# Transposes of the normalized rows by transfers and VectorE, in a macaron block of FFN, linear attention and FFN

## The chip, the cores and the metric

The kernel runs on one core of one Trainium2 chip. The metric is the device time of one execution in microseconds (us); times given are medians over runs.

## What is computed

The input is x, 4096 tokens of 256 features (two sequences of 2048). The reference, cut to what matters:

```
x = x + 0.5 * ffn(layernorm(x))          # FFN stage 1
x = x + attn(layernorm(x))               # linear attention, 16 heads of 16
x = x + 0.5 * ffn(layernorm(x))          # FFN stage 2

ffn(x):  x_prev = x shifted by one token
         xr = mu_r*x + (1-mu_r)*x_prev ;  xk = mu_k*x + (1-mu_k)*x_prev
         return sigmoid(xr @ W_r.T) * (square(relu(xk @ W_k.T)) @ W_v.T)
attn(x): q = relu(x Wq)/4 ; k = relu(x Wk)/4 ; v = x Wv ; u = silu(x Wu)
         kv = sum over tokens of k v, per head ; out = q kv
         return (head_norm(out) * u) @ Wo.T
```

## The kernel before

The tokens are cut into 8 blocks of 512 (4 tiles of 128 tokens). `FFN` numbers the work: n = 0 to 7 is stage 1 on block n, n = 8 to 15 is stage 2 on block n - 8. There is no scheduler: each engine's program is written out by hand, in order, and engines wait for one another only by semaphores. So an instruction that waits holds back all that stands behind it on its engine.

The change lies in the loops `for i in range(1, 7)` that every engine has. Iteration i does the projections of FFN i, prepares the mixed rows of FFN i+1, and does the attention projections of block i-1. TensorE (PE) does in iterations 2 to 6: `ffn_k(i)`, `transpose_a(i+1)`, `transpose_b(i-1)`, `ffn_r(i)`, `k_and_u(i-1)`, `ffn_v(i)`, `gram(i-1)` and `q_of(i-1)`; from i = 5 on also `attend`, in i = 6 `transpose_g(0)` and `project_out(0)`. Every product is three fp32r matmuls (high by high, low by high, high by low), so each operand needs a high and a low part, which other engines make.

What the steps of the prediction touch:

- `transpose_a(n)` (L1300, L1310): eight 128x128 transposes on PE from the normalized rows `xn` (tokens on partitions) to PSUM `psA` (features on partitions). ScalarE's `previous(n)` (L636, L642) and VectorE's `mix_current(n)` (L957) read `psA`.
- The rows of `xn` come from ScalarE's `normalize(n)` (L625), which waits for `s_lnA >= 3*n`, that is for GpSimd's `scales_a(n)` (L405 to L417: `var_epsA`, `rstdA`, `mean_rstdA`, `shiftA`). Its statistics are VectorE's `stats_a(n)` (`bn_rows`, `bn_all`).
- ScalarE in iteration i: `front` = `activate_k(i)` (relu and square of both halves, L685, L692), `x2_high(i-1)` (L720), `previous(i+1)`, `sigmoid_r`, `mix_high`; then `sigmoid_u` four times (L739, L746) with two `kt_high` (L730), `mix_high(i+1, 1)`, `normalize(i+2)`, `x1_high`, `relu_q`.
- VectorE in iteration i: `stats_a(i+2)`, `x2_low(i-1)` (L1033), `mix_current(i+1)`, four `silu` (L1039), then `gate_ffn`/`add_ffn1` twice (L1020, L1027), `stats_b(i)` (L948, L951), `r_low`, `keep_g`; from i = 5 on `gate_heads` and `head_norms` (the Newton steps, L1099 to L1119).
- GpSimd (POOL) in iteration i: `act_low(i)` (L446, L455), `k_low(i+1)` (L433), `kt_low(i-1)` (L485), `scales_a(i+2)`, `scales_b(i)` (L421 to L426, waits for `stats_b(i)`), `x1_low(i)` (L476); in i = 2 also `wo_lo` (L552).
- `gram(i-1)` on PE waits for the two halves of `kt_low`, the second one at its third tile (L1463). `k_and_u(i-1)` waits for `x2_low`; `project_out(0)` waits for VectorE's `g_low(0)` (L1047).
- SyncE (SP) loads x and the weights, then stores: `load_x`, `store_x`.

## Time and profile before

| | |
|---|---|
| time, median of 3 runs | 312.24 us (310.92 to 312.5) |
| the profiled execution | 310.67 us, its span 308.9 us |
| granted TensorE clock | 1.00 throughout |
| PE, PEld (weight load) busy | 301.8 us (98%), 275.2 us (89%) |
| VectorE, ScalarE, GpSimd busy | 240.9 (78%), 235.5 (76%), 215.1 (70%) |
| DMA | 10.85 MB, nearly all before 20 us and after 230 us |

The page gives the busy time of each engine and its share of the span; a busy share is a mean over stages. Which wait ends last in a stage is read from the instructions in order of time, and times in those rows are in us from the span's start. The profiled execution took 1.8 us more than its span.

### The profile page before, as it was taken

How to read it: one execution, taken by the hardware profiler on the slowest of the kernel's cores; microseconds unless marked ns; L12 is line 12 of the kernel's file. 1: busy time of each engine (PE TensorE's matmuls, PEld its weight loads, DVE VectorE, ACT ScalarE, POOL GpSimd, SP SyncE). 2: the span in 40 equal slices, each digit the busy share in tenths (PEclk: the TensorE clock that was granted, in tenths of full speed). 3: DMA queues.
4: the chain of work that ended last, by engine and by line, in shares of the span. 5: the costliest groups of instructions: out<-in, count | busy, mean ns of one | idle time of the engine just before them, and what ended most of it. 6: DMA issues, size and time to landing. Idle time of an engine off the chain costs nothing.

```text
span 308.9 us, 5806 instructions
## 1 busy us (share of the span) xinstructions
PE 301.8 (98%) x2035; PEld 275.2 (89%) x2035; DVE 240.9 (78%) x585; ACT 235.5 (76%) x461; POOL 215.1 (70%) x237
## 2 busy tenths in 40 slices
PE   6999999999999999999999999999999999999995
PEld 4888889988988998998988998989999999999984
DVE  5899875666856946985994799596989797999695
ACT  3979669699589679679269358579797979699981
POOL 4598978789687686669278315726797979758823
PEclk9999999999999999999999999999999999999999
DMA  7960000000000000000000000000001011101123
GB/s 217 382 217 3 0 1 2 2 0 0 3 0 3 0 0 2 0 2 0 0 3 1 2 0 0 2 1 3 0 3 68 11 59 36 35 2 68 39 100 136
DMA packets 10752, 10.85 MB, mean 35 GB/s; under 512 B 482, under 2 KB 10724, under 8 KB 10724
## 3 DMA queue, kind: packets, MB, share of 16 engines
q1 hardware_dynamic: 10432, 10.23, 9.6%
q8 instruction: 16, 0.26, 0.4%
q10 hardware_dynamic: 292, 0.26, 0.2%
q14 instruction: 12, 0.10, 0.1%
HBM read 6.29 MB, written 4.19 MB: 34 GB/s over the span
## 4 chain that ended last, share of the span: by engine, by line
PE 74%; DVE 14%; ACT 4%; POOL 3%; issue 2%; DMA 1%; DVEq 0%; ACTq 0%
PE psK L1293 7%; PE psK L1295 7%; PE psK L1294 7%; PE psX L1293 7%; PE psX L1295 7%; PE psX L1294 7%; PE psRV L1293 6%; PE psRV L1294 6%; PE psRV L1295 6%; DVE mix L957 3%; PE psA L1310 3%; PE psA L1498 2%; PE psX L1511 2%; PE psX L1425 2%; PE psK L1498 2%
## 5 line engine op out<-in xcount | busy, mean ns | idle before, releaser
L957 DVE SCALAR_TENSOR_TENSOR mix<-psA,mu,mix 128x512 f32<-128x512 f32 x60 | 41.5, 745 | 10.0 <-ACT mix L642 10.0
L625 ACT ACTIVATE xn<-xs,shiftA,rstdA 128x256 f32<-128x256 f32 x53 | 27.7, 607 | 16.3 <-POOL shiftA L417 16.3
L433 POOL TENSOR_TENSOR mix_k_lo<-mix,mix_k_hi 128x512 fp32r<-128x512 f32 x26 | 33.2, 1299 | 8.2 <-ACT mix_k_hi L675 8.2
L642 ACT ACTIVATE mix<-psA,one_mu 128x511 f32<-128x511 f32 x60 | 36.9, 697 | 0.0
L1293 PE MATMUL psRV<-ffn_hi,mix_r_hi 128*128 128x256 f32 x120 | 34.3, 286 | 0.0
L1295 PE MATMUL psRV<-ffn_hi,mix_r_lo 128*128 128x256 f32 x120 | 33.6, 280 | 0.0
L1294 PE MATMUL psRV<-ffn_lo,mix_r_hi 128*128 128x256 f32 x120 | 33.5, 279 | 0.0
L1293 PE MATMUL psRV<-ffn_hi,act_hi 128*128 128x256 f32 x96 | 27.5, 287 | 0.2 <-POOL act_lo L455 0.2
L1294 PE MATMUL psRV<-ffn_lo,act_hi 128*128 128x256 f32 x96 | 26.8, 280 | 0.0
L1295 PE MATMUL psRV<-ffn_hi,act_lo 128*128 128x256 f32 x96 | 26.8, 279 | 0.0
L485 POOL TENSOR_TENSOR k_lo<-k_tok,k_hi 128x512 fp32r<-128x512 f32 x14 | 18.1, 1292 | 11.5 <-ACT k_hi L730 11.5
L926 DVE BATCH_NORM_STATS2 statsA<-xs 128x6 f32<-128x256 f32 x64 | 22.5, 415 | 2.5 <-DMA xs<-x_dram 2.4
L1293 PE MATMUL psK<-mix_k_hi,ffn_hi 128*128 128x512 f32 x60 | 24.2, 403 | 0.0
L476 POOL TENSOR_TENSOR x_lo<-xs,x_hi 128x512 fp32r<-128x512 f32 x14 | 17.8, 1295 | 8.6 <-ACT x_hi L725 8.6
L1295 PE MATMUL psK<-mix_k_hi,ffn_lo 128*128 128x512 f32 x60 | 23.6, 393 | 0.0
L1294 PE MATMUL psK<-mix_k_lo,ffn_hi 128*128 128x512 f32 x60 | 23.4, 391 | 0.0
L1293 PEld LDWEIGHTS psRV<-ffn_hi,mix_r_hi 128*128 128x128 f32 x120 | 22.5, 188 | 0.5 <-issue 0.2
L1294 PEld LDWEIGHTS psRV<-ffn_lo,mix_r_hi 128*128 128x128 f32 x120 | 22.6, 188 | 0.2
L1295 PEld LDWEIGHTS psRV<-ffn_hi,mix_r_lo 128*128 128x128 f32 x120 | 22.5, 187 | 0.0
L1033 DVE TENSOR_TENSOR x_lo<-psX,x_hi 128x512 fp32r<-128x512 f32 x16 | 10.3, 685 | 14.4 <-ACT x_hi L720 14.4
L675 ACT ACTIVATE mix_k_hi<-mix 128x512 fp32r<-128x512 f32 x30 | 19.0, 660 | 1.9 <-DVE mix L957 1.8
L1293 PEld LDWEIGHTS psRV<-ffn_hi,act_hi 128*128 128x128 f32 x96 | 18.0, 188 | 0.7 <-POOL act_lo L455 0.4
(210 smaller groups left out, 1081.3 us busy)
## 6 DMA issues: line engine op xcount, KB each, us to landing
xs<-x_dram SPq DMA_DIRECT2D x7, 512.0 KB, 7.8
out_dram<-xs SPq DMA_DIRECT2D x7, 512.0 KB, 2.9
out_dram<-xs SPq DMA_DIRECT2D x4, 128.0 KB, 1.8
xs<-x_dram ACTq DMA_DIRECT2D x2, 128.0 KB, 2.8
xs<-x_dram SPq DMA_DIRECT2D x2, 128.0 KB, 2.6
silu_u<-w_ffn_k_dram SPq DMA_DIRECT2D x1, 256.0 KB, 4.7
silu_u<-w_ffn_r_dram SPq DMA_DIRECT2D x1, 256.0 KB, 5.8
q_store<-w_k_dram SPq DMA_DIRECT2D x1, 256.0 KB, 6.0
```

The source lines that it names most:

```text
L433: nc.gpsimd.tensor_tensor(mix_k_lo[:, h, :], mix[:, 0, h, :], mix_k_hi[:, h, :].bitcast(F32), ALU.subtract).then_inc(s_lo_k, 1)
L476: nc.gpsimd.tensor_tensor(x1_lo[:, g * BANK:(g + 1) * BANK], row(xs, a, g * BANK, BANK), x1_hi[:, g * BANK:(g + 1) * BANK].bitcast(F32), A ...
L485: nc.gpsimd.tensor_tensor(k_lo[:, tiles, :], k_tok[:, tiles, :], k_hi[:, tiles, :].bitcast(F32), ALU.subtract).then_inc(s_kt_lo, 1)
L625: nc.scalar.activation(xn[:, t, :], tile_row(xs, b, t), ACT.Identity, bias=shiftA[:, t:t + 1], scale=rstdA[:, t:t + 1]).then_inc(s_xn, 1)
L642: nc.scalar.activation(mix[:, rk, h, 1:BLOCK], psA[:, h, 0:BLOCK - 1], ACT.Copy, scale=one_mu[:, rk, h:h + 1]).then_inc(s_prev, 1)
L675: nc.scalar.activation(hi[:, h, :], mix[:, rk, h, :], ACT.Identity).then_inc(done, 1)
L926: nc.vector.bn_stats(statsA[:, t, :], tile_row(xs, b, t)).then_inc(s_bnA, 1)
L957: nc.vector.scalar_tensor_tensor(out=m, in0=psA[:, h, :], scalar=mu[:, rk, h:h + 1], in1=m, op0=ALU.mult, op1=ALU.add).then_inc(s_mix, 1)
L1293: nc.tensor.matmul(dst, a_hi, b_hi, start=start, stop=False)
L1294: nc.tensor.matmul(dst, a_hi, b_lo, start=False, stop=False)
L1295: return nc.tensor.matmul(dst, a_lo, b_hi, start=False, stop=stop)
L1498: last = nc.tensor.matmul(ps[:, t // 2, (t % 2) * D + h * P:(t % 2) * D + (h + 1) * P], q_half(j, h)[:, tok(t)], kv_bd[:, j // BB, h, :], ...
```

## The change

For n = 3 to 7 `transpose_a(n)` is gone from PE. In its place:

- SyncE waits for the normalized rows of n (and, for n = 4 to 6, for the transposes of n-1 by VectorE; for n = 7 for the weight means) and issues 16 transfers that move 32-row bands of the rows to other partitions, each 32 partitions x 8 x 32 elements. They land in `squares` (n < 7) or `wsum` (n = 7).
- VectorE's new `turn(n)` waits for them and does two 32x32-block transposes of 128x512 into `psA`. For n = 3 it stands behind `x2_low(1)` in iteration 2, for n = 4 to 6 at the head of iteration n-1, for n = 7 at the end of iteration 5.
- The normalized rows of n = 4 and 6 are written to `gout` instead of `xn`.
- Statistics of n = 5 to 7 move one iteration earlier on VectorE: the four `bn_stats` stand between the `silu` calls, `bn_all` behind `stats_b`.
- GpSimd: `scales_a(i+2)` stands ahead of `act_low(i)` for i = 2 to 5 (for i = 1 between `act_low(1)` and `k_low(2)`). `act_low(6)` now stands ahead of `norm_second(0)`.
- ScalarE: for i = 2 to 6 `x2_high` stands between the two halves of `activate_k(i)`. `normalize(4)` stands behind them in iteration 2, ahead of `previous`. In iterations 3 to 5 tiles 0 and 1 of `normalize(i+2)` stand ahead of `activate_k(i)` and tiles 2 and 3 behind it.
- VectorE's `head_norms(0)` moves from the end of iteration 5 to iteration 6, between `x2_low(5)` and `mix_current(7)`; only its sums stay in iteration 5.

```diff
+        TURNED = range(3, 8)
+        QUAD = 32
+        QUADS = P // QUAD
...
+        def turned_before(n):
+            return 2 * n - 2 * (n in TURNED and n > TURNED[0])
@@ block.sync
+            for n in TURNED:
+                sp.wait_ge(*normalized(n, TILES - 1))
+                if n == 7:
+                    sp.wait_ge(s_wmean, 4)
+                elif n > TURNED[0]:
+                    sp.wait_ge(s_tA, 2 * n)
+                for j in range(QUADS):
+                    for i in range(QUADS):
+                        rows = quads_of(n)[j * QUAD:(j + 1) * QUAD, i * D:(i + 1) * D]
+                        sp.dma_start(rows.rearrange("c (th f) -> c th f", f=QUAD),
+                                     rows_of(n)[i * QUAD:(i + 1) * QUAD, :, :].rearrange(
+                                         "c t (h j f) -> c (t h) j f", h=HALVES, j=QUADS)[:, :, j, :]
+                                     ).then_inc(s_quads[n % 2], 16)
@@ block.gpsimd
             for i in range(1, 6):
+                if i > 1:
+                    scales_a(i + 2)
                 act_low(i)
+                if i == 1:
+                    scales_a(3)
                 k_low(i + 1)
                 if i > 1:
                     kt_low(i - 1)
-                scales_a(i + 2)
                 scales_b(i)
                 x1_low(i)
...
+            act_low(6)
             norm_second(0)
-            act_low(6)
@@ block.scalar, front(i, nxt, a)
-                activate_k(i)
-                if a is not None and i > 1:
+                    activate_k(i)
+                else:
+                    if i in (3, 4, 5):
+                        normalize(i + 2, (0, 1))
+                    activate_k(i, (0,))
                     x2_high(a)
+                    activate_k(i, (1,))
+                    if i == 2:
+                        normalize(4)
+                    elif i < 6:
+                        normalize(i + 2, (2, 3))
...
-                if i <= 5:
-                    normalize(i + 2)
+                if i == 1:
+                    normalize(3)
@@ block.vector
+            def turn(n, free=()):
+                for s, v in free:
+                    dve.wait_ge(s, v)
+                dve.wait_ge(s_halo, n + 1)
+                dve.wait_ge(s_quads[n % 2], 16 * QUADS * QUADS * ((n - TURNED[0]) // 2 + 1))
+                blocks = quads_of(n).rearrange("p (i t h f) -> p h t i f", i=QUADS, t=TILES, h=HALVES)
+                for h in range(HALVES):
+                    nc.vector.transpose(psA[:, h, :].rearrange("p (t i c) -> p t i c", t=TILES, i=QUADS),
+                                        blocks[:, h, :, :, :]).then_inc(s_tA, 1)
...
-                if 1 < i <= 5:
-                    stats_a(i + 2)
+                if i == 2:
+                    stats_a(4)
+                if 3 <= i <= 5:
+                    turn(i + 1, {4: [(s_wcen, 4)], 5: [(s_kvbd, 1)]}.get(i, ()))
                 if i > 1:
                     x2_low(i - 1)
+                if i == 2:
+                    turn(3)
+                if i == 6:
+                    head_norms(0, True)
                 mix_current(i + 1)
...
-                projections(i - 1)
+                projections(i - 1, i + 3 if 2 <= i <= 4 else None)
...
                 stats_b(i)
+                if 2 <= i <= 4:
+                    bn_all(i + 3)
...
-                    head_norms(i - 5)
+                if i == 5:
+                    for g in range(2):
+                        head_sums(0, g)
+                    turn(7, [(s_gu, 2)])
+                elif i == 6:
+                    head_norms(1)
@@ block.tensor
-                transpose_a(i + 1, [(s_wcen, 4)] if i == 4 else [])
...
-            transpose_a(6, [(s_kvbd, 1)])
...
-            transpose_a(7, [(s_gu, 2)])
```

How the order moves at two places. ScalarE, from the end of iteration 2 into iteration 3, before (`q_store` is `relu_q(1)`, `act_k` and `act_hi` are `activate_k(3)`, `x_hi<-psX` is `x2_high(2)`, `mix` is `previous(4)`):

```order
L752 ACTIVATE q_store<-psX 128x512 [waits s_q] x2
L685 ACTIVATE act_k<-psK 128x512 [waits s_act_lo,s_k]
L692 ACTIVATE act_hi<-act_k 128x512 [waits s_v,s_relu]
L685 ACTIVATE act_k<-psK 128x512 [waits s_k]
L692 ACTIVATE act_hi<-act_k 128x512 [waits s_relu]
L720 ACTIVATE x_hi<-psX 128x512 [waits s_q,s_tB]
L720 ACTIVATE x_hi<-psX 128x512 [waits s_tB]
L636 ACTIVATE mix<-halo 128x4 [waits s_halo,s_lo_r,s_lo_k]
```

and the same place in the changed kernel:

```order
L787 ACTIVATE q_store<-psX 128x512 [waits s_q] x2
L660 ACTIVATE xn<-xs,shiftA,rstdA 128x256 [waits s_tA,s_lnA]
L660 ACTIVATE xn<-xs,shiftA,rstdA 128x256
L720 ACTIVATE act_k<-psK 128x512 [waits s_act_lo,s_k]
L727 ACTIVATE act_hi<-act_k 128x512 [waits s_v,s_relu]
L755 ACTIVATE x_hi<-psX 128x512 [waits s_q,s_tB]
L755 ACTIVATE x_hi<-psX 128x512 [waits s_tB]
L720 ACTIVATE act_k<-psK 128x512 [waits s_k]
L727 ACTIVATE act_hi<-act_k 128x512 [waits s_relu]
L660 ACTIVATE xn<-xs,shiftA,rstdA 128x256 [waits s_tA,s_lnA]
L660 ACTIVATE xn<-xs,shiftA,rstdA 128x256
L671 ACTIVATE mix<-halo 128x4 [waits s_halo,s_lo_r,s_lo_k]
```

Two tiles of `normalize(5)` with their wait for `s_lnA` now stand ahead of `activate_k(3)`, two behind it and ahead of `previous(4)`.

GpSimd, from the end of iteration 2 into iteration 3, before (`var_epsB` to `rstd2B` is `scales_b(2)`, `x_lo` is `x1_low(2)`, then `act_low(3)`):

```order
L421 TENSOR_SCALAR var_epsB<-meanvarB 128x4 [waits s_aggB]
L424 TENSOR_TENSOR rstdB<-var_epsB,minus_half 128x4 [waits s_mvB]
L426 TENSOR_TENSOR rstd2B<-rstdB 128x4 [waits s_lnB]
L476 TENSOR_TENSOR x_lo<-xs,x_hi 128x512 [waits s_x1hi] x2
L552 TENSOR_TENSOR wo_lo<-wo,wo_hi 128x512 [waits s_wo_hi]
L446 TENSOR_TENSOR act_k<-act_k 128x512 [waits s_act_hi] x2
```

and in the changed kernel:

```order
L453 TENSOR_SCALAR var_epsB<-meanvarB 128x4 [waits s_aggB]
L456 TENSOR_TENSOR rstdB<-var_epsB,minus_half 128x4 [waits s_mvB]
L458 TENSOR_TENSOR rstd2B<-rstdB 128x4 [waits s_lnB]
L508 TENSOR_TENSOR x_lo<-xs,x_hi 128x512 [waits s_x1hi] x2
L587 TENSOR_TENSOR wo_lo<-wo,wo_hi 128x512 [waits s_wo_hi]
L440 TENSOR_SCALAR var_epsA<-meanvarA 128x4 [waits s_aggA]
L445 TENSOR_TENSOR rstdA<-var_epsA,minus_half 128x4 [waits s_xn,s_mvA]
L447 TENSOR_TENSOR mean_rstdA<-meanvarA,rstdA 128x4 [waits s_lnA]
L449 TENSOR_SCALAR shiftA<-mean_rstdA 128x4 [waits s_lnA]
L478 TENSOR_TENSOR act_k<-act_k 128x512 [waits s_act_hi] x2
```

`scales_a(5)`, whose last instruction writes `shiftA`, now stands behind `scales_b(2)`, `x1_low(2)` and `wo_lo`, ahead of `act_low(3)`.

## Rows read from the trace of the kernel before

**Rows 1.** The page: granted clock in 40 slices, and the chain that ended last, by engine
```profile
PEclk9999999999999999999999999999999999999999
...
PE 74%; DVE 14%; ACT 4%; POOL 3%; issue 2%; DMA 1%; DVEq 0%; ACTq 0%
```

**Rows 2.** Iterations 2, 4, 6 (length; PE, PEld, DVE, ACT, POOL busy; clock)
```profile
43.78:64.99 21.21, 21.21 (x137) 19.05 (x136) 13.34 (x33) 16.83 (x34) 16.17 (x17) 1.00 0.01 2
...
86.86:109.14 22.28, 22.28 (x145) 20.02 (x145) 14.15 (x34) 17.73 (x35) 16.61 (x18) 1.00 0.00 1
...
132.24:158.96 26.72, 26.72 (x185) 24.63 (x184) 21.91 (x52) 17.35 (x34) 15.88 (x15) 1.00 0.01 2
```

**Rows 3.** TensorE in order of time, iteration 2: start us, length us, engine, line
```profile
46.51 1.04 PE L1310 MATMUL psA<-ident,xn 128*128 128x128 f32 x8
47.38 1.04 PE L1425 MATMUL psX<-ident,xs 128*128 128x128 f32 x8
```

**Rows 4.** ScalarE in order of time, iteration 2 (idle time and its releaser in brackets)
```profile
45.34 0.60 ACT L685 ACTIVATE act_k<-psK 128x512 f32<-128x512 f32 x1 [0.76 <-PE psK L1295]
45.97 0.63 ACT L692 ACTIVATE act_hi<-act_k 128x512 fp32r<-128x512 f32 x1
...
48.02 1.09 ACT L720 ACTIVATE x_hi<-psX 128x512 fp32r<-128x512 f32 x2
48.98 0.21 ACT L636 ACTIVATE mix<-halo 128x4 f32<-128x4 f32 x1
...
56.78 0.47 ACT L739 ACTIVATE k_tok<-psK,rstd2B 128x256 f32<-128x256 f32 x1 [0.48 <-PE psK L1295]
57.16 0.47 ACT L746 ACTIVATE silu_u<-psK,rstdB 128x256 f32<-128x256 f32 x1
57.51 0.63 ACT L730 ACTIVATE k_hi<-k_tok 128x512 fp32r<-128x512 f32 x1
...
61.90 2.08 ACT L625 ACTIVATE xn<-xs,shiftA,rstdA 128x256 f32<-128x256 f32 x4 [2.72 <-POOL shiftA L417]
```

**Rows 5.** VectorE in order of time, iteration 2
```profile
57.66 0.48 DVE L1039 SCALAR_TENSOR_TENSOR silu_u<-psK,rstdB,silu_u 128x256 f32<-128x256 f32 x1 [0.83 <-ACT silu_u L746]
58.20 0.69 DVE L1020 SCALAR_TENSOR_TENSOR gate<-psRV,gate 128x512 f32<-128x512 f32 x1
```

**Rows 6.** GpSimd in order of time, iteration 2
```profile
58.22 1.30 POOL L485 TENSOR_TENSOR k_lo<-k_tok,k_hi 128x512 fp32r<-128x512 f32 x1 [1.27 <-ACT k_hi L730]
59.60 0.52 POOL L408 TENSOR_SCALAR var_epsA<-meanvarA 128x4 f32<-128x4 f32 x1
...
63.20 0.55 POOL L421 TENSOR_SCALAR var_epsB<-meanvarB 128x4 f32<-128x4 f32 x1 [1.33 <-DVE meanvarB L951]
...
65.39 2.55 POOL L476 TENSOR_TENSOR x_lo<-xs,x_hi 128x512 fp32r<-128x512 f32 x2
67.89 1.28 POOL L552 TENSOR_TENSOR wo_lo<-wo,wo_hi 128x512 fp32r<-128x512 f32 x1
```

**Rows 7.** TensorE in order of time, end of iteration 5
```profile
124.89 0.28 PE L1293 MATMUL psK<-k_hi,x_hi 128*128 128x256 f32 x1
...
127.71 1.95 PE L1498 MATMUL psA<-kv_bd,q_store 128*128 128x128 f32 x16
```

**Rows 8.** VectorE in order of time, end of iteration 5 and iteration 6
```profile
132.79 1.27 DVE L1099 SCALAR_TENSOR_TENSOR head_ss<-var_epsB,head_ss 128x64 f32<-128x64 f32 x1
...
137.11 1.29 DVE L1033 TENSOR_TENSOR x_lo<-psX,x_hi 128x512 fp32r<-128x512 f32 x2 [0.28 <-ACT x_hi L720]
...
147.13 1.29 DVE L1047 TENSOR_TENSOR g_lo<-psX,g_hi 128x512 fp32r<-128x512 f32 x2 [0.52 <-ACT g_hi L768]
```

**Rows 9.** DMA issues: engine, count, KB each, median us from issue to landing
```profile
out_dram<-xs SPq DMA_DIRECT2D x7, 512.0 KB, 2.9
out_dram<-xs SPq DMA_DIRECT2D x4, 128.0 KB, 1.8
```

**Rows 10.** SyncE's queue in order of time: start, length of one issue
```profile
3.22 0.47 SPq L369 DMA_DIRECT2D q_store<-w_k_dram  x1
```

More of the change, by code:

```diff
@@ L168, in macaron @@
         s_tA = sem("s_tA")
+        s_quads = [sem(f"s_quads_{k}") for k in range(2)]
         s_prev = sem("s_prev")
@@ L294, in prev_part, with quads_of, rows_of @@
             return mix_part(n, rk, h) + n
+        TURNED = range(3, 8)
+        QUAD = 32
+        QUADS = P // QUAD
+        def quads_of(n):
+            return (squares[:].rearrange("p g e -> p (g e)") if n < 7
+                    else wsum[:].rearrange("p n e -> p (n e)"))
+        def rows_of(n):
+            return gout if n in TURNED and n % 2 == 0 else xn
+        def turned_before(n):
+            return 2 * n - 2 * (n in TURNED and n > TURNED[0])
         def half(g):
@@ L620, in normalize @@
                 if n > 0:
-                    act.wait_ge(s_tA, 2 * n)
+                    act.wait_ge(s_tA, turned_before(n))
                 for t in tiles:
@@ L624, in normalize @@
                         continue
-                    nc.scalar.activation(xn[:, t, :], tile_row(xs, b, t), ACT.Identity,
+                    nc.scalar.activation(rows_of(n)[:, t, :], tile_row(xs, b, t), ACT.Identity,
                                          bias=shiftA[:, t:t + 1], scale=rstdA[:, t:t + 1]).then_inc(s_xn, 1)
@@ L1186, in _, with projections @@
             ffn_weight_low(2)
-            def projections(a):
+            def projections(a, n=None):
                 for t in range(TILES):
+                    if n is not None:
+                        bn_rows(n, (t,))
                     silu(a, t)
             for i in range(1, 7):
-                if 1 < i <= 5:
-                    stats_a(i + 2)
+                if i == 2:
+                    stats_a(4)
+                if 3 <= i <= 5:
+                    turn(i + 1, {4: [(s_wcen, 4)], 5: [(s_kvbd, 1)]}.get(i, ()))
                 if i > 1:
                     x2_low(i - 1)
+                if i == 2:
+                    turn(3)
+                if i == 6:
+                    head_norms(0, True)
                 mix_current(i + 1)
```

## The prediction

> **What bounds the kernel now.** I read the page first: the chain that ended last runs 74% on PE, at full granted clock [rows 1]. The stretches of iterations 2, 4 and 6 come next: PE is busy for all of each, and they last 21.21, 22.28 and 26.72 us [rows 2]; their edges give the starts of iterations 2, 4 and 6 (43.78, 86.86 and 132.24 us). So PE binds, and every instruction taken from it shortens the kernel, but only while the others keep up. Their own order of time is what matters then. ScalarE runs from 45.34 to 58.14 in iteration 2 with a single idle spot that a wait on PE makes, 0.48 us at 56.78; its large idle time, 2.72 us, lies just before `normalize`, where it waits for `shiftA` [rows 4]. GpSimd works through `k_lo`, `scales_a`, `scales_b`, `x_lo` and `wo_lo` [rows 6]. The reader should see that the wait for `shiftA` stood where ScalarE had time to spare.
>
> **What is taken from PE.** Eight transposes take 47.38 - 46.51 = 0.87 us [rows 3]. Five blocks give 5 x 0.87 = 4.35 us, all of it on the path as long as nobody else is late. That is the most the change can win.
>
> **The transfers.** 80 of them, 16 for each block. One issue on SyncE takes 0.47 us [rows 10], so 16 take 7.5 us; the last lands 1.8 us later if it takes as long as a store of 128 KB [rows 9]: 9.3 us. Their pieces are 32 elements, 128 bytes, 4096 of them for 512 KB, eight times as many as in a store of the same 512 KB (rows of 256 elements), which took 2.9 us. If time goes by pieces this is at most 8 x 2.9 = 23.2 us; if by bytes, 2.9 us and the issues bind. I take 9.3 us, since each issue is a short row and the store is the nearest one. `normalize(3)` keeps its place in iteration 1; one iteration before 61.90 + 2.08 [rows 4] is 42.8, and its `scales_a` no longer stands behind two low parts of 1.3 us [rows 6], so its rows are ready near 40 us (an estimate), and `turn(3)` can start near 49: just covered. At 23.2 us `turn(3)` would be 14 us late, once; later blocks have some 20 us each, by the times below, so the cover holds for them or is short by little.
>
> **VectorE's new work.** Ten block transposes of 128x512. The trace shows none; the cheapest 128x512 row is about 0.65 us, twice that is the upper end: 1.4 to 2.7 us for a pair [nearest: rows 5, `gate`, 0.69]. I take 1.4. They lie where VectorE waited for `x2_high`, so I cost them at nothing; without that cover it would be 1.4 us an iteration. The statistics between the `silu` calls fill gaps such as the 0.83 us before 57.66 [rows 5].
>
> **What the moved steps do.** In iterations 3 to 5 the first two tiles of `normalize(i+2)` stand ahead of `activate_k(i)` on ScalarE, and wait for `shiftA`. On GpSimd `scales_a(i+2)` now stands behind `x1_low(i-1)`. In the old trace GpSimd leaves `x1_low(2)` at 67.89 and `wo_lo` at 69.17 [rows 6], while iteration 3 starts at 64.99, the end of the stretch of iteration 2 [rows 2]. So `shiftA` comes several us after the point where ScalarE used to begin `activate_k` (1.56 us into iteration 2: 45.34 against 43.78 [rows 2, 4]). All that ScalarE does for PE stands behind it.
>
> First `shiftA(5)`, on the old clock. Relu and square of half 0 from 45.34; `x2_high(1)` starts 0.64 us into `transpose_b`, as before (48.02 - 47.38), which now begins at 46.51: 47.15. It takes 0.96 (to 48.98), half 1 takes 1.27 (0.64 + 0.63), all four tiles of `normalize(4)` 2.0: `previous(3)` starts at 51.38 instead of 48.98 [rows 3, 4]. From there to the end of the last sigmoid was 57.63 - 48.98 less the 0.48 idle: 8.17 us, dense, so 59.55. Then `silu` to `gate` 0.57 (58.20 - 57.63) [rows 5]; `gate` to `scales_b` 5.00 (63.20 - 58.20); `scales_b` 2.19; `x1_low` 2.50; `wo_lo` 1.23 to 1.28; `scales_a` 2.30 (61.90 - 59.60) [rows 4, 6]. Sum: 73.3 us.
>
> Then each `shiftA` follows from the one before, round a loop of three engines, none of which has idle time in it:
>
> normalize two tiles 1.0 + half 0 1.27 + `x2_high` 0.96 + half 1 1.27 + two tiles 1.0 + `previous` to last sigmoid 8.17 + 0.57 + 5.00 + 2.19 + 2.50 + 2.30 = 26.2 us.
>
> Two rounds: `shiftA(7)` at 73.3 + 52.4 = 125.7. From it the end of iteration 5: 5.5 us (the first five terms) to `previous(6)`, 8.68 to the end of the second `kt_high` (58.14 - 48.98, less 0.48, plus rounding), 0.08 + 1.30 for the second `kt_low` [rows 4, 6], then PE's last three quarters of `gram` (3/4 of 127.71 - 124.89 = 2.12) and `attend` with `q_of`, 132.24 - 127.71 = 4.53 [rows 2, 7]: 125.7 + 5.5 + 8.68 + 1.38 + 2.12 + 4.53 = 147.9. Iteration 6 thus begins 15.7 us late (132.24 before). The four times 0.87 us that PE has saved by then are in that figure: PE now waits.
>
> **Iteration 6** has no `normalize`. It saves its 0.87 us but `head_norms(0)` now stands ahead of `mix_current(7)` on VectorE. The steps filled 132.79 to 136.83 (137.11 less 0.28 idle), 4.0 us, of which the first took 1.27 us where its twins take 0.2 to 0.3: 3.0 to 4.0 [rows 8]. `x2_low` now ends 2.73 + 0.64 + 0.63 + 1.29 = 5.3 us into the iteration (`transpose_b` at 2.73, the rest as in [rows 3, 4, 8]), so the mix starts at 8.3 to 9.3. From the end of `x2_low` to the end of `g_low` it was 148.42 - 138.40 = 10.0 us, about 0.9 of it waiting (0.52 at `g_low` itself): 9.1, so `g_low` ends at 17.4 to 18.4. PE reached `project_out` when `g_low` was ready, 16.2 to 16.5 us in, and comes 0.87 earlier now, at 15.6: a stall of 1.8 to 2.8, a net loss of 0.9 to 1.9. I take 1.3. Moving `norm_second(0)` behind `act_low(6)` costs nothing: PE needs it only after `k_and_u`.
>
> **Sum.** 15.7 + 1.3 = 17 us. The profiled execution took 310.67 us, so 327.7; the median of the runs shown is 1.6 us above it, which gives 329.
>
> **Where the Trainium skill bears on it.** A store of 128 KB took 1.8 us from issue to landing [rows 9]. The Trainium skill, DMA: Bandwidth & Descriptors, Rules for kernel authors, says that under 64 KB one pays mostly overhead and should coalesce small transfers; each one here is 32 KB. By that rule this change is the wrong way round; the trace agrees only as far as 128 KB takes 1.8 us where 512 KB takes 2.9. It gives rival B below. In the trace the clock stands at 1.00 with PE never idle [rows 1, 2]. The Trainium skill, TensorE: Matmul & The Clock Gate, Why this matters for your kernels, warns that idle gaps of PE bring the clock back down; no run here shows it, and it gives rival C.
>
> **The rivals.**
> A, faster: `scales_a` comes early enough that ScalarE never waits. Its statistics are indeed ready an iteration sooner. It decides at the point where `shiftA` comes no later than 1.0 us ahead of the old start of `activate_k`, 0.6 us into the iteration. Then the 4.35 us stay: 310.67 - 4.35 = 306.3, 307.9 as a median. Against it stand the rows of GpSimd: it leaves `x1_low` 2.9 us into iteration 3 and needs 2.3 more. Chance 0.04.
> A', the delay comes once and does not go round the loop, because engines behind it have slack that I don't see: some 5 us at iteration 3 and 2 at iteration 2, less 4.35: 310.67 + 2.65 + 1.6 = 315. Chance 0.04.
> B, the transfers do not overlap: 16 x 1.8 = 28.8 us for each block. Then the loop runs through transfers and `turn`, 28.8 + 1.4 = 30.2 us for each of n = 4 to 7, and `turn(3)` is at 40 + 28.8 = 68.8, done at 70.2. `turn(7)` comes at 70.2 + 4 x 30.2 = 191, where I expect it near 150: 40 us more, 369. Half-way cases (23.2 us a block) cost `turn(3)` some 13 us: 342. Chance 0.09 together.
> C, the clock falls to its lower level (1.2 GHz) in the gaps that PE now has, about 26.2 - (22.28 - 0.87) = 4.8 us in each of iterations 3 to 5. Most of the slower matmuls are hidden in the loop; only the last 6.65 us of iteration 5 are on the path, and as much again in iteration 6: up to 7 us more, 333 to 336. Chance 0.09.
>
> **How the numbers follow.** Forecast 0.74: 329 us, own range 323 to 335 (1 us for iteration 6, the rest for what of the loop is looser or tighter than its rows, four rounds at 1 us). A and A' lie below 318, B above 338; C lies inside. Range 318 to 338. A measurement here can tell 0.5% (1.6 us) from no change. Faster 0.04 (A), same 0.02 (between A and A'), slower 0.94.
>
> **What would show it.** `shiftA` of blocks 5, 6 and 7 some 26 us apart; ScalarE's largest wait at `normalize` for `shiftA`, about 4 to 6 us, three times; PE idle before `k_and_u` in iteration 3 for `x2_low` and before the third tile of `gram` for `k_lo`; iterations 3 to 5 at 25 to 28 us instead of 22 to 23; the transfers of a block landed within 10 us. I am wrong if ScalarE does not wait there, if VectorE waits for the transfers, or if the granted clock falls.

## The result, and the profile after

| | before | changed |
|---|---|---|
| median (lowest to highest), us | 311.58 (310.41 to 312.5) | 331.54 (330.66 to 332.14) |
| ratio, 95% interval | 1 | 1.0641 [1.0592, 1.0689] |
| profiled execution / its span, us | 310.67 / 308.9 | 331.65 / 329.9 |

The changed kernel is 6.4% slower; the forecast was 329, with a range of 318 to 338. Of all the runs below one is left out, of the kernel with the Newton steps back: 338.75 us at a mean granted clock of 0.849, against 324.67 to 325.4 us in its others. The changed kernel's page answers to [rows 1]: TensorE's clock shows two dips, and only half of the chain that ended last is TensorE's.

```profile
PE 305.6 (93%) x1995; PEld 275.8 (84%) x1995; DVE 250.1 (76%) x595; ACT 235.3 (71%) x461; POOL 213.6 (65%) x237
PEclk9999999998999999999979999999999999999999
...
PE 49%; DVE 17%; ACT 15%; POOL 9%; issue 5%; SPq 3%; DMA 1%; POOLq 0%; ACTq 0%; DVEq 0%
```

Iterations 2 to 6 as stretches, cut where TensorE begins `ffn_k(i)` (columns as in [rows 2]; the third figure is the length):

```profile
46.04:70.37 24.33, 21.36 (x128) 18.43 (x128) 17.06 (x45) 18.15 (x36) 16.68 (x21) 1.00 0.22 37
70.37:97.52 27.15, 22.89 (x131) 19.87 (x131) 16.00 (x38) 17.18 (x35) 17.41 (x19) 0.94 0.12 20
97.52:123.18 25.66, 22.22 (x137) 19.32 (x137) 15.32 (x36) 17.04 (x34) 15.94 (x18) 1.00 0.13 22
123.18:148.61 25.43, 22.96 (x148) 20.37 (x147) 15.84 (x32) 17.40 (x35) 15.69 (x18) 1.00 0.13 21
...
148.61:180.16 31.55, 27.51 (x178) 25.20 (x176) 25.25 (x55) 17.27 (x34) 15.96 (x15) 0.95 0.00 1
```

Iterations 3 and 5 of the kernel before, from the view of [rows 2]:

```profile
64.99:86.86 21.87, 21.87 (x139) 19.44 (x139) 14.76 (x36) 18.09 (x36) 17.86 (x21) 1.00 0.01 1
...
109.14:132.24 23.10, 23.10 (x155) 21.07 (x154) 16.50 (x39) 17.61 (x35) 16.54 (x18) 1.00 0.00 1
```

Before, the five lasted 21.21, 21.87, 22.28, 23.10 and 26.72 us, 115.18 together; now 134.12. That is 18.9 of the 21.0 us between the spans. The rest is in front: iteration 1 began at 22.86 us here and at 20.75 in the execution shown of before. It began near 22.9 in 3 of the 14 profiled executions of this study and between 20.6 and 21.1 in the others, so I put these 2 us down to the execution and not to the change. How many of the timed runs began late is not known. Below, kernels are compared by the sum of iterations 2 to 6 in their traces, and by the timed runs.

ScalarE in order of time at the head of iterations 3, 4 and 5, where [rows 4] had `act_k` at once:

```profile
69.92 0.60 ACT L787 ACTIVATE q_store<-psX 128x512 f32<-128x512 f32 x1 [0.63 <-PE psX L1363]
76.07 1.09 ACT L660 ACTIVATE xn<-xs,shiftA,rstdA 128x256 f32<-128x256 f32 x2 [5.55 <-POOL shiftA L449]
77.07 0.57 ACT L720 ACTIVATE act_k<-psK 128x512 f32<-128x512 f32 x1
...
101.35 1.09 ACT L660 ACTIVATE gout<-xs,shiftA,rstdA 128x256 f32<-128x256 f32 x2 [4.29 <-POOL shiftA L449]
...
126.63 1.09 ACT L660 ACTIVATE xn<-xs,shiftA,rstdA 128x256 f32<-128x256 f32 x2 [4.29 <-POOL shiftA L449]
```

GpSimd, which makes `shiftA`:

```profile
68.37 0.19 POOL L453 TENSOR_SCALAR var_epsB<-meanvarB 128x4 f32<-128x4 f32 x1 [3.68 <-DVE meanvarB L994]
...
70.22 2.55 POOL L508 TENSOR_TENSOR x_lo<-xs,x_hi 128x512 fp32r<-128x512 f32 x2
72.71 1.30 POOL L587 TENSOR_TENSOR wo_lo<-wo,wo_hi 128x512 fp32r<-128x512 f32 x1
74.09 0.20 POOL L440 TENSOR_SCALAR var_epsA<-meanvarA 128x4 f32<-128x4 f32 x1
...
75.84 0.19 POOL L449 TENSOR_SCALAR shiftA<-mean_rstdA 128x4 f32<-128x4 f32 x1
...
101.12 0.19 POOL L449 TENSOR_SCALAR shiftA<-mean_rstdA 128x4 f32<-128x4 f32 x1
...
126.40 0.20 POOL L449 TENSOR_SCALAR shiftA<-mean_rstdA 128x4 f32<-128x4 f32 x1
```

From `shiftA` of block 5 to that of block 6, and from there to that of block 7, it is 25.28 us, twice to the hundredth. That is how a closed loop without idle time looks. TensorE stands behind it. Its longest waits in the whole span (total in us, times, longest), apart from one of 2.6 us at the very start that the kernel before has too:

```profile
PE psX L1361 <- DVE x_lo L1086: 5.4, 3, 3.2
PE psK L1361 <- POOL k_lo L517: 5.0, 6, 1.0
PE psX L1579 <- DVE silu_u L1092: 4.0, 1, 4.0
```

The third is not of the loop: `transpose_g(0)` in iteration 6 waits for the `silu` products, behind the Newton steps. Nor are the losses of iteration 2 (3.1 us), where ScalarE normalizes the four tiles of block 4 ahead of `previous(3)` and TensorE then waits 1.00 and 0.95 us for `k_lo` and 0.53 us for a sigmoid. No experiment changes this place alone; in the versions a block ahead, which do not have it, iteration 2 lasts 21.3 us.

### The profile page after: what moved, and what is told of

Read it like the earlier page. It is cut to its first block, busy times and chain, and to the rows that moved or that the text cites. A ratio compares the mean times of both kernels' runs of the same rounds, so it can differ in the third digit from the quotient of the medians.

```text
span 329.9 us, 5823 instructions
## 1 busy us (share of the span) xinstructions
PE 305.6 (93%) x1995; PEld 275.8 (84%) x1995; DVE 250.1 (76%) x595; ACT 235.3 (71%) x461; POOL 213.6 (65%) x237
## 4 chain that ended last, share of the span: by engine, by line
PE 49%; DVE 17%; ACT 15%; POOL 9%; issue 5%; SPq 3%; DMA 1%; POOLq 0%; ACTq 0%; DVEq 0%
PE psX L1361 4%; PE psX L1363 4%; PE psX L1362 4%; PE psK L1361 4%; PE psRV L1361 4%; PE psK L1363 4%; PE psRV L1363 4%; PE psK L1362 4%; PE psRV L1362 4%; SPq L406 3%; ACT mix L677 3%; ACT xn L660 2%; POOL x_lo L508 2%; PE psA L1566 2%; DVE mix L1000 2%
## 5 line engine op out<-in xcount | busy, mean ns | idle before, releaser
L660 ACT ACTIVATE xn<-xs,shiftA,rstdA 128x256 f32<-128x256 f32 x45 | 23.8, 610 | 12.5 <-POOL shiftA L449 12.5
L1361 PE MATMUL psRV<-ffn_hi,act_hi 128*128 128x256 f32 x96 | 28.4, 296 | 0.8 <-ACT gate L748 0.5
L1362 PE MATMUL psRV<-ffn_lo,act_hi 128*128 128x256 f32 x96 | 27.5, 287 | 0.0
L1363 PE MATMUL psRV<-ffn_hi,act_lo 128*128 128x256 f32 x96 | 27.5, 286 | 0.0
L1086 DVE TENSOR_TENSOR x_lo<-psX,x_hi 128x512 fp32r<-128x512 f32 x16 | 10.3, 684 | 21.3 <-ACT x_hi L755 21.3
L969 DVE BATCH_NORM_STATS2 statsA<-xs 128x6 f32<-128x256 f32 x64 | 23.4, 414 | 2.3 <-DMA xs<-x_dram 2.1
L478 POOL TENSOR_TENSOR act_k<-act_k 128x512 f32<-128x512 f32 x14 | 14.5, 1046 | 13.3 <-ACT act_hi L727 13.3
L453 POOL TENSOR_SCALAR var_epsB<-meanvarB 128x4 f32<-128x4 f32 x8 | 2.9, 368 | 31.1 <-DVE meanvarB L994 31.1
```

The costliest lines, as they stand in the source:

```text
L478: nc.gpsimd.tensor_tensor(act_k[:, h, :], act_k[:, h, :], act_k[:, h, :], ALU.mult).then_inc(s_sq, 1)
L660: nc.scalar.activation(rows_of(n)[:, t, :], tile_row(xs, b, t), ACT.Identity, bias=shiftA[:, t:t + 1], scale=rstdA[:, t:t + 1]).then_inc(s ...
L969: nc.vector.bn_stats(statsA[:, t, :], tile_row(xs, b, t)).then_inc(s_bnA, 1)
L1361: nc.tensor.matmul(dst, a_hi, b_hi, start=start, stop=False)
L1362: nc.tensor.matmul(dst, a_hi, b_lo, start=False, stop=False)
L1363: return nc.tensor.matmul(dst, a_lo, b_hi, start=False, stop=stop)
```

## The experiments

"Sum" is iterations 2 to 6 in the trace. Before: 115.18; the changed kernel: 134.12.

| kernel | median, us | ratio to before, 95% | sum, us |
|---|---|---|---|
| rows behind | 325.12 | 1.0453 [1.0416, 1.0490] | 129.34 |
| scales first | 323.27 | 1.0384 [1.0344, 1.0424] | 126.31 |
| both | 325.45 | 1.0451 [1.0391, 1.0510] | 127.95 |
| TensorE's transposes | 331.16 | 1.0647 [1.0595, 1.0700] | 134.52 |
| Newton steps back | 324.72 | 1.0447 [1.0397, 1.0496] | 129.88 |
| Newton steps alone | 314.26 | 1.0115 [1.0060, 1.0170] | 117.96 |
| scales first, Newton steps back | 316.37 | 1.0196 [1.0158, 1.0235] | 120.18 |
| a block ahead, 4 to 6 | 309.16 | 0.9948 [0.9921, 0.9975] | 112.68 |
| a block ahead, 4 to 7 | 307.84; again 308.02 | 0.9925 [0.9892, 0.9958]; 0.9918 [0.9893, 0.9944] | 111.94; 111.84 |
| the same, TensorE's transposes | 311.27 | 1.0028 [1.0009, 1.0048] | 114.97 |
| the same, turned twice | 309.30 | 0.9965 [0.9946, 0.9983] | 113.37 |

("GELU" in the recorded expectations stands for `activate_k`, which is relu and square.)

### Is it the transposes or the order?

```diff
-                if 3 <= i <= 5:
-                    turn(i + 1, {4: [(s_wcen, 4)], 5: [(s_kvbd, 1)]}.get(i, ()))
...
+                transpose_a(i + 1, [(s_wcen, 4)] if i == 4 else [])
```

(and so for n = 3, 6 and 7; SyncE's 80 transfers go.)

> Edit: the order of the changed kernel on all engines, but TensorE transposes the rows of blocks 3 to 7 as in the kernel before: no transfers, no transposes on VectorE. Theory (the order costs, not the way of transposing): TensorE has 4.35 us more work, but most of it in iterations in which it waits, so the time is 329 to 335 us, far above 311.6. Rival (the transfers and VectorE's transposes are what costs): the time falls to 310 to 318 us.

331.16 us, as slow as the changed kernel. ScalarE waits 5.53 us for `shiftA` at the head of iteration 3, where it waited 5.55, and the three `shiftA` again lie 25.28 and 25.27 us apart. Transfers, transposes on VectorE and the 4.35 us taken from TensorE together make no difference that can be measured in this order. The rival is refuted: the order costs the whole of it.

### The loop, cut in two ways

Rows behind:

```diff
-                    if i in (3, 4, 5):
-                        normalize(i + 2, (0, 1))
                     activate_k(i, (0,))
                     x2_high(a)
                     activate_k(i, (1,))
-                    if i == 2:
-                        normalize(4)
-                    elif i < 6:
-                        normalize(i + 2, (2, 3))
+                    if i < 6:
+                        normalize(i + 2)
```

> Edit: in iterations 3 to 5 ScalarE normalizes no tile of block i+2 ahead of its GELU of block i; all four tiles come behind it. Theory (the time went into an ordered loop ScalarE - VectorE - GpSimd that comes back to itself through shiftA): the two tiles ahead hold the GELU back by a wait for shiftA of 4 to 6 us and by 1.0 us of work. Without them the loop falls from the 25.3 us measured between two shiftA to about 22.7, so iterations 4 and 5 take 22 to 24 us on TensorE where they took 27.2 and 25.7, and the time is 321 to 326 us, against 331.5 of the changed kernel. Rival (the transfers or VectorE's transposes of the rows cost the time): the transfers start no earlier, the time stays at 329 to 333. Rival (the loop closes another way, for instance through x2_low): the waits move to another wait on GpSimd, and the time falls by under 3 us.

Scales first, on GpSimd:

```diff
             for i in range(1, 6):
-                if i > 1:
-                    scales_a(i + 2)
+                if i == 2:
+                    scales_a(4)
                 act_low(i)
...
                 scales_b(i)
+                if 2 <= i <= 4:
+                    scales_a(i + 3)
                 x1_low(i)
```

> Edit: GpSimd makes the scales of block i+2 directly behind scales_b of the block before, ahead of that iteration's x1_low and wo_lo parts. Theory (loop through shiftA): the 2.5 us of x1_low (and 1.2 of wo_lo) leave the stretch between the previous sigmoid and shiftA; the loop falls from 25.3 to 22 to 23.7 us, ScalarE's wait for shiftA falls from 4 to 6 us to 1 to 3, and the time is 320 to 326 us. Rival (transfers): the rows are ready 2 to 3 us earlier each block, so the time would fall only if turn() was waited for; it was waited for only in the first block, so 329 to 333. Rival (what is pushed back, x2_low, decides): TensorE's wait for x2_low before k_and_u grows and the time stays within 2 us.

325.12 and 323.27 us: 6.4 and 8.3 us less than the changed kernel, with the transfers as they were. In scales first the row on which the theory rests reads

```profile
70.32 1.09 ACT L662 ACTIVATE xn<-xs,shiftA,rstdA 128x256 f32<-128x256 f32 x2 [1.81 <-POOL shiftA L449]
```

where the changed kernel waited 5.55. Both show that the loop through `shiftA` held TensorE. With the rows behind, iterations 4 and 5 took 24.17 and 24.30 us, just over the 22 to 24 expected. (The 27.2 and 25.7 us in that expectation are those of iterations 3 and 4.)

> Edit: both of the above together. Theory: the loop comes to about 20 us, which is under the 21 to 22 us that TensorE itself needs for an iteration, so shiftA is waited for by nobody in iterations 4 and 5, TensorE's iterations 3 to 5 take 21 to 23 us (27.2, 25.7 and 25.4 before), iteration 6 starts at 135 to 139 us in place of 148.6, and the time is 317 to 322 us: what is left over the kernel before is iteration 2 and 3's loss and that of iteration 6. Rival (transfers cost the time): 327 or more. If it comes to the two singles' gains added (some 14 us off) the two were separate delays; if to much less than the sum, TensorE or another engine bounds from about 22 us on.

325.45 us: the expectation failed. With both edits ScalarE no longer waits for `shiftA` in iterations 3 to 5, and yet iterations 4 and 5 last 24.16 and 24.32 us, 1 us more than with scales first alone (its two below):

```profile
93.94:118.10 24.16, 21.94 (x136) 19.26 (x137) 15.32 (x36) 17.15 (x34) 15.90 (x18) 1.00 0.14 23
118.10:142.42 24.32, 22.70 (x147) 20.31 (x146) 15.82 (x32) 17.52 (x35) 15.94 (x17) 1.00 0.14 22
```

```profile
91.77:114.95 23.18, 21.73 (x136) 19.21 (x137) 15.31 (x36) 17.05 (x34) 15.92 (x18) 1.00 0.15 24
114.95:138.27 23.32, 22.43 (x148) 20.24 (x146) 15.83 (x32) 17.52 (x35) 15.96 (x17) 1.00 0.14 23
```

ScalarE of both, in order of time, iteration 4:

```profile
95.63 0.60 ACT L722 ACTIVATE act_k<-psK 128x512 f32<-128x512 f32 x1 [2.14 <-PE psK L1361]
...
99.58 2.07 ACT L662 ACTIVATE gout<-xs,shiftA,rstdA 128x256 f32<-128x256 f32 x4
...
109.41 0.68 ACT L767 ACTIVATE k_hi<-k_tok 128x512 fp32r<-128x512 f32 x1
```

and TensorE, which waits at `gram` for GpSimd's `k_lo`, made from that `k_hi`:

```profile
109.61 0.36 PE L1359 MATMUL psK<-k_hi,x_hi 128*128 128x256 f32 x1 [0.68 <-POOL k_lo L517]
111.49 0.39 PE L1359 MATMUL psK<-k_hi,x_hi 128*128 128x256 f32 x1 [0.96 <-POOL k_lo L517]
```

I read this as a second loop, which I had not seen: `ffn_k`, `act_k`, all that ScalarE does up to the last `k_hi` (nearly dense from 95.63 to 110.09), `k_lo`, `gram`, `g_acc`, `ffn_k`. Its parts add up: 1.69 us to `act_k`, 14.46 on ScalarE, 1.40 to the second half of `gram` at 111.49, 6.61 on TensorE to the next `ffn_k` at 118.10, together 24.16. Rows behind alone has the same iterations 3 to 5 (23.84, 24.17 and 24.30 us against 23.83, 24.16 and 24.32), so there too this loop and not `shiftA` held TensorE: once the rows stand behind, making the scales earlier gains nothing. In scales first only two tiles lie inside this loop, but the first loop is still closed: ScalarE waits about 1.8 us for `shiftA` three times, and the three lie 22.80 and 22.81 us apart. Its 23.2 us are thus no clean measure of the second loop with two tiles. Two tiles ahead of `act_k` would fall into the time in which ScalarE waits for TensorE anyway (2.14 us above) if `shiftA` came early enough; that was not run. By this reading rows do least harm in front of or behind the whole stretch; the versions a block ahead bear it out.

### The Newton steps

Back to the end of iteration 5:

```diff
-                if i == 6:
-                    head_norms(0, True)
                 mix_current(i + 1)
...
                     turn(7, [(s_gu, 2)])
+                    head_norms(0, True)
```

> Edit: in the changed kernel the first heads' Newton steps go back to the end of iteration 5, behind the transposes of block 7's rows. Theory (the steps, placed ahead of mix_current(7), hold up the silu products of block 6 and with them TensorE's transpose_g: iteration 6 took 31.6 us where it took 26.7 before): iteration 6 falls to 26.5 to 28 us, the wait of 4.04 us for silu_u and the low clock behind it go, and the time is 326 to 329 us against 331.5. Rival (iteration 6 is long because block 7 comes late through shiftA): it stays at 30 us or more, and the time at 330 or more. Rival (prediction's size, 0.9 to 1.9 us): 329.6 to 330.6.

The other way round, in the kernel before:

```diff
                 if i > 1:
                     x2_low(i - 1)
+                if i == 6:
+                    head_norms(0, True)
                 mix_current(i + 1)
...
-            norm_second(0)
             act_low(6)
+            norm_second(0)
```

(`head_norms(0)` keeps its sums in iteration 5.)

> Edit: the kernel before, with only the second part of the change: the first heads' Newton steps in iteration 6 behind x2_low(5) and ahead of mix_current(7), and GpSimd's low parts of the activation ahead of the second part of the norms. Theory (the loss of iteration 6 is this step's own, 3.5 to 5 us): 314.7 to 316.6 us against 311.4. Rival (it is the prediction's 0.9 to 1.9 us, and the rest came from the blocks being late): 312.3 to 313.3. Rival (in the order of before the steps are hidden): 310.5 to 312.

Back: 324.72 us, 6.8 less, and below the 326 to 329 expected. Iterations 5 and 6 last 26.93 and 26.29 us in place of 25.43 and 31.55, 3.8 together; TensorE waits for no `silu_u`, and its granted clock in iteration 6 is 1.00 again. In iteration 5 it fell, behind two waits for `k_lo`, of 0.58 and 0.95 us, which the changed kernel has too (0.58 and 0.94) and which show no dip there:

```profile
138.00:142.00 4.00, 3.05 (x18) 2.86 (x18) 3.90 (x7) 0.91 (x2) 1.22 (x1) 0.75 0.26 42
```

The clock is 0.75 in these 4 us and 0.83 in the next 4, which is 1.7 us of full clock, enough for the 1.5 us by which iteration 5 is longer; what set it off is open. By the traces the steps' place costs 3.8 us (iterations 5 and 6 together) to 5.3 us (iteration 6 alone). Of the 6.25 us between the two profiled executions 4.2 lie in iterations 2 to 6 and 2.0 in the later start; the rest of the timed difference can be of that kind. Alone: 314.26 us against 310.61 in the same runs, 3.65 more (expected: 314.7 to 316.6), and 3.03 in iteration 6 (29.75). VectorE in that kernel:

```profile
131.22 1.27 DVE L1081 TENSOR_REDUCE head_ss<-squares 128x32 f32<-128x512 f32 x2
136.84 1.29 DVE L1033 TENSOR_TENSOR x_lo<-psX,x_hi 128x512 fp32r<-128x512 f32 x2 [4.36 <-ACT x_hi L720]
138.05 0.58 DVE L1099 SCALAR_TENSOR_TENSOR head_ss<-var_epsB,head_ss 128x64 f32<-128x64 f32 x1
...
142.32 2.72 DVE L957 SCALAR_TENSOR_TENSOR mix<-psA,mu,mix 128x512 f32<-128x512 f32 x4
```

The 4.36 us that it now waits are the hole that the steps used to fill [rows 8: 132.79 to 136.83]. Behind `x2_low` the same steps have no hole, so the mix begins at 142.32 instead of 138.85, and TensorE stops at `transpose_g(0)`:

```profile
147.57 1.09 PE L1517 MATMUL psX<-ident,gout 128*128 128x128 f32 x8 [2.68 <-DVE silu_u L1039]
```

That settles it: this part of the change costs 3 us or more by itself, in either order. (The edit moves the steps and GpSimd's `act_low(6)` together, as the change does; they were not tried apart.) The two causes add: with scales first and the steps back the traces' sum is 120.18, and the time

> Edit: the changed kernel with GpSimd's scales directly behind scales_b (323.3 us by itself) and with the Newton steps at the end of iteration 5 (325.1 us by itself). Theory (two separate causes, which add): 331.5 - 8.2 - 6.5 = 316.8, so 315.5 to 318 us. What is then left over the kernel before is iteration 2's and 3's loss and what the GELUs behind normalized tiles still cost. Rival (the Newton steps then stand in front of work that the faster loop wants early): 318.5 or more.

316.37 us, as expected. What is left over the kernel before sits in iterations 2 to 4 (23.78, 23.36 and 23.18 us against 21.21, 21.87 and 22.28).

### What the transposes are worth where the order does no harm

The version a block ahead: in the kernel before, every step that prepares a block's rows keeps its slot but works on the next block:

```diff
-                scales_a(i + 2)
+                if i + 3 <= 7:
+                    scales_a(i + 3)
...
-                if i <= 5:
-                    normalize(i + 2)
+                if i + 3 <= 7:
+                    normalize(i + 3)
...
-                projections(i - 1)
+                projections(i - 1, i + 3 if i + 3 <= 7 else None)
...
+                if 3 <= i <= 5:
+                    turn(i + 1, {4: [(s_wcen, 4)], 5: [(s_kvbd, 1)]}.get(i, ()))
...
                     gate_heads(i - 5)
+                    if i == 5:
+                        turn(7, [(s_gu, 2)])
                     head_norms(i - 5)
```

Block 3 stays with TensorE and is normalized and scaled in iteration 1; `projections` takes the next block's `bn_stats` between its `silu` calls; transfers and `turn` are the changed kernel's.

> Edit: the kernel before, in which the rows of blocks 4 to 6 are transposed by transfers and VectorE, and their statistics, scales and normalization run one block further ahead in the slots that they had, so that nothing that waits for shiftA stands ahead of a GELU; the Newton steps as before. Theory (the transfers and VectorE's transposes are harmless; the order cost the time): TensorE is rid of 3 times 0.87 us and waits for nothing new: 307.5 to 310.5 us against 311.4. Rival (the transposes on VectorE, 1.3 us a block, or the issues on the transfer queue delay something in any order): 311 to 315. Rival (a gap in which TensorE did the transposes just opens): 311 to 312.

> Edit: as the one for blocks 4 to 6, with block 7 as well, its VectorE transposes behind gate_heads(0). Theory (as there): another 0.87 us less for TensorE, less up to 0.6 us by which VectorE's work of iteration 6 starts later: 306.5 to 310 us. Rival (the end of iteration 5 and iteration 6 have no room on VectorE for the two transposes of 1.3 us): slower than the version for blocks 4 to 6 by 0.5 to 1.5 us.

309.16 and 307.84 us: both faster than the kernel before, by 0.5% and 0.75%. TensorE has no new wait above 0.2 us (iterations 2 to 6 of the second):

```profile
44.05:65.38 21.33, 21.33 (x136) 19.16 (x137) 14.11 (x35) 18.36 (x39) 17.46 (x19) 1.00 0.15 25
65.38:86.47 21.09, 20.95 (x131) 18.55 (x130) 15.69 (x38) 17.96 (x37) 17.87 (x21) 1.00 0.16 26
86.47:107.99 21.52, 21.45 (x136) 19.14 (x137) 15.09 (x36) 17.41 (x35) 16.60 (x18) 1.00 0.16 27
107.99:130.15 22.16, 22.16 (x148) 20.19 (x147) 16.07 (x32) 15.55 (x31) 14.75 (x14) 1.00 0.14 23
130.15:155.99 25.84, 25.84 (x178) 23.79 (x177) 22.25 (x55) 17.12 (x34) 15.70 (x15) 1.00 0.00 1
```

ScalarE still waits 2.71 us for `shiftA` in iteration 3, but behind the last `k_hi`, where nobody waits for it:

```profile
82.82 2.08 ACT L662 ACTIVATE gout<-xs,shiftA,rstdA 128x256 f32<-128x256 f32 x4 [2.71 <-POOL shiftA L449]
```

Three runs beside each other then separate order and transposes: the same order with TensorE's transposes, the same with VectorE's done twice, and the version itself again.

```diff
                 for h in range(HALVES):
                     nc.vector.transpose(psA[:, h, :].rearrange("p (t i c) -> p t i c", t=TILES, i=QUADS),
+                                        blocks[:, h, :, :, :]).then_inc(s_twice, 1)
+                dve.wait_ge(s_twice, HALVES * (n - TURNED[0] + 1))
+                for h in range(HALVES):
+                    nc.vector.transpose(psA[:, h, :].rearrange("p (t i c) -> p t i c", t=TILES, i=QUADS),
                                         blocks[:, h, :, :, :]).then_inc(s_tA, 1)
```

> Edit: the order of the version for blocks 4 to 7 (statistics, scales and normalization one block further ahead), but TensorE does all transposes: no transfers, none on VectorE. Theory (moving a transpose off TensorE is worth its 0.87 us where TensorE has no gap, and the order itself is worth nothing): 3.5 us above the version with transfers, so 310.5 to 312 us, like the kernel before. Rival (the order, not the transposes, gave the 2.8 us): 307 to 309 us.

> Edit: the version for blocks 4 to 7 in which VectorE transposes each block's two halves twice over, 1.4 us more of VectorE for each of four blocks. Theory (VectorE has room there: it is busy 60 to 75 per cent of those iterations, and TensorE waits for nothing of it): within 0.7 us of the same version without the doubling, with at most the mix of the block coming 1.4 us later. Rival (VectorE's transposes are on the path to mix_current): 1.4 us for each block, some 5 us more.

> Edit: none against the version for blocks 4 to 7, run again beside the three others for a closer figure. Theory: 306.5 to 309 us, and faster than the kernel before by 0.4 to 1.2 per cent. Rival (the first figure of 0.9925 was chance): a ratio of 0.997 to 1.003.

With TensorE's transposes 311.27 us, again 308.02: 3.25 us for four blocks, of 4 x 0.87 = 3.48 possible. The order itself gives nothing: with TensorE's transposes it is 0.28% slower than the kernel before, just clear of noise, and iteration 1, which now prepares block 4 as well, lasts 23.3 us instead of 23.0. The gain of 0.8% is no chance.

Turned twice is 1.3 us slower than the version itself, where I expected at most 0.7. The place is single: iterations 3 to 5 are unchanged (21.12, 21.54, 22.22), iteration 6 lasts 27.14 instead of 25.62 to 25.84, where TensorE now waits 1.08 us for `x2_low`, behind `turn(7)` and the Newton steps. So for blocks 4 to 6 VectorE had 1.3 us free; for block 7 it has none. The expectation had taken VectorE as busy for 60 to 75% of these iterations; in iteration 6 it is busy for 22.25 of 25.84 us.

## Why the prediction was right

**The bound and the gain from TensorE.** TensorE was the bound, and a transposed block is worth its 0.87 us while nobody else is late; shown at 3.25 of 3.48. In the changed kernel the 4.35 us are worth nothing, as said ("PE now waits"). That the loop through `shiftA` would outlast TensorE's own round, and by how much, was right, and it is the larger part of the loss: iteration 6 began 14.3 us late with this execution's start taken off.

**The transfers.** The rows of block 3 were ready near 41 (39 by the start of before), forecast 40. An issue takes longer than the 0.47 us of [rows 10]. SyncE's queue in order of time, and VectorE's first `turn`:

```profile
41.16 11.54 SPq L406 DMA_DIRECT2D squares<-xn  x16
55.50 10.38 SPq L406 DMA_DIRECT2D squares<-gout  x16
...
54.09 1.32 DVE L1010 STREAM_TRANSPOSE psA<-squares 128x512 f32<-128x512 f32 x2 [2.63 <-DMA squares<-xn]
```

Sixteen take 10.4 to 11.5 us, 0.65 to 0.72 each, and a transfer lands 1.9 us after its issue (median): 12 to 13 us a block, not 9.3, inside the bounds of 2.9 and 23.2. The same queue had issues of 0.43 to 0.93 us in the kernel before, so the one row of 0.47 was a narrow basis. `turn(3)` was therefore not "just covered" but waited 2.63 us; that iteration lasts 24.08 us with TensorE's transposes too, so it cost at most 0.25. With that two signs of the list went against the prediction: the transfers did not land within 10 us, and VectorE waited for them, once. Rival B is refuted: the transfers overlap. The Trainium skill (DMA: Bandwidth & Descriptors, Rules for kernel authors) advises against transfers under 64 KB as mostly overhead. The trace agrees as far as the issuing queue goes, which these transfers hold for 0.65 to 0.72 us each. In the versions a block ahead they cost nothing: the same table's advice to issue early and wait late is what these versions do.

**VectorE's transposes.** A pair took 1.32 us, forecast 1.4, hidden.

**`shiftA(5)`** was to be ready at 73.3 us; it was at 76.03, of which 2.1 are the later start of this execution: 73.9.

**The loop** was put at 26.2 us; it is 25.28. Most of that is GpSimd's: `scales_a` takes 1.95 us (from 124.65 to 126.60) for the 2.30 of the sum and `scales_b` 1.85 for 2.19, since their first instructions (`var_epsA`, `var_epsB`) now take 0.19 where [rows 6] had 0.52 and 0.55. **Iteration 6** began at 148.61, or 146.5 with this execution's start taken off, forecast 147.9.

**Iteration 6 itself** is the term that was mis-sized: a net loss of 0.9 to 1.9 us was forecast, "I take 1.3"; it was 4.8. I had the steps at 3.0 to 4.0 us and TensorE's stall at `project_out`. VectorE in order of time:

```profile
153.80 0.21 DVE L1152 SCALAR_TENSOR_TENSOR head_ss<-var_epsB,head_ss 128x64 f32<-128x64 f32 x1
...
154.54 0.95 DVE L1160 SCALAR_TENSOR_TENSOR head_t<-head_t,head_ss 128x64 f32<-128x64 f32 x1
155.52 1.23 DVE L1162 SCALAR_TENSOR_TENSOR head_y<-head_t,head_y 128x64 f32<-128x64 f32 x1
156.79 1.23 DVE L1164 TENSOR_TENSOR head_t<-head_y 128x64 f32<-128x64 f32 x1
...
159.44 2.72 DVE L1000 SCALAR_TENSOR_TENSOR mix<-psA,mu,mix 128x512 f32<-128x512 f32 x4
```

The steps took 5.6 us, from 153.80 to 159.44. That is the mis-sized term: three of these instructions took 0.95, 1.23 and 1.23 us where the others take 0.2, 2.7 us more in all. Each ended 0.1 us behind a pass of GpSimd that was under way when it began (`act_low(6)`, beside which the change puts them):

```profile
154.28 1.12 POOL L478 TENSOR_TENSOR act_k<-act_k 128x512 f32<-128x512 f32 x1 [1.74 <-ACT act_hi L727]
155.37 2.57 POOL L487 TENSOR_TENSOR act_lo<-act_k,act_hi 128x512 fp32r<-128x512 f32 x2
```

From the start of the mix to the end of `g_low` (168.42) it took 9.0 us, where the forecast had 9.1. So by the forecast's own path `g_low` ended 19.8 us into the iteration instead of 17.4 to 18.4, a stall of 4.2 us and a net loss of 3.3 instead of 1.3. The other 1.5 us are the clock, to which the forecast gave nothing (rival C, below). TensorE also stopped in another place, at `transpose_g(0)`, for 4.04 us; I had followed the chain from the mix to `g_low`, and not asked which of TensorE's instructions first reads anything made behind the mix. In time this made no difference by itself: with `ffn_v(6)` at its old length TensorE would have reached `project_out` at 168.44, when `g_low` was ready.

The forecast of 329 came near to 331.5 by some luck: iteration 6 cost 3.5 us more than forecast, the loop 0.9 us a round less.

**The rivals.** A and A' are refuted: ScalarE waited 4.3 to 5.6 us three times, once a round, as in the list of signs. C was half right, and the list has a falling clock as a sign of being wrong. TensorE's granted clock over the stretches behind its two long waits (the first figure behind the engines' busy times is the clock):

```profile
80.00:84.00 4.00, 3.74 (x10) 2.96 (x11) 1.43 (x3) 4.00 (x9) 3.50 (x3) 0.57 0.10 17
...
164.00:168.00 4.00, 3.32 (x20) 3.32 (x21) 2.33 (x5) 4.00 (x11) 2.57 (x2) 0.71 0.02 4
168.00:172.00 4.00, 4.00 (x32) 4.00 (x32) 3.53 (x6) 0.62 (x2) 0.00 (x0) 0.86 0.00 0
```

0.57 is near half of full speed, the lower of its two levels, 1.2 GHz of 2.4, for most of that stretch. TensorE had stood still for 3.17 us before the first dip and for 4.04 before the second. Its shorter waits (up to 1.32 us) show no dip in this trace, though two of 0.58 and 0.95 us do in iteration 5 of the kernel with the Newton steps back; and the one of 2.68 us in the kernel with the Newton steps alone shows none. So the warning of the Trainium skill (TensorE: Matmul & The Clock Gate, Why this matters for your kernels) that idle gaps bring the clock down agrees with this trace, though the length of one gap does not tell here whether a dip follows. In iteration 3 it cost nothing, since the loop was slower still; in iteration 6, where TensorE was the bound again, `ffn_v(6)` took 4.45 us instead of 2.91. That is some 1.5 us on the path, not the up to 7 of the rival.

## What to carry to other kernels

Work taken from the busiest engine is worth its time only if the steps that replace it keep their places relative to what that engine waits for: prepare the data a whole round earlier in the old slot, rather than in the same round in front of something urgent. A wait set in front of an engine's urgent work is worth a look for the loop it closes: follow it once round through all engines, add the durations, and compare with the bound's own round. A step that fills another engine's hole is free only there, so before moving it, find the hole, what the other engines do beside the new place (here GpSimd's passes made the steps 2.7 us longer), and the first instruction of the bound engine that depends on anything behind it.

## What was not expected of the hardware

- Sixteen 32 KB transfers between partitions keep the issuing queue for 10.4 to 11.5 us, yet the DMA engines are busy only 12 to 22% of these iterations; the 128-byte pieces cost no more than that here.
- VectorE transposes 128x512 of 4 bytes from SBUF into PSUM, in blocks of 32x32, in 0.70 us each (lowest 0.68, highest 0.73 of eight in the version a block ahead). A block needs two, 1.32 us with their overlap, against the 0.87 us that its eight 128x128 transposes take on TensorE.
- The same 128x64 VectorE instructions take 0.2 us or up to 1.27. In the rows above the long ones end at 155.49, 156.75 and 158.02, each 0.1 us behind a 128x512 pass of GpSimd that ran when they began (ends 155.40, 156.66 and 157.94). In the kernel before one of 1.27 from 132.79 ends at 134.06, behind `x_lo` on GpSimd (to 133.97); the kernel with the Newton steps back has 0.60 (to 149.28, `x_lo` to 149.19) and 1.02 (to 151.60, `act_k` to 151.52). In the 14 traces, from 126 to 252 us, 37 such instructions take over 0.3 us, and every one of them ends within 0.12 us behind such a pass. One that began together with a pass stayed at 0.22 (154.28), and those beside GpSimd's 128x4 instruction `rstdA` of 1.01 us stay below 0.3. No run was made to separate this from other causes.
